# Expert weight loads in eight paced pieces each, with the slot loads between them

## What is computed

```python
xf = layernorm(x).reshape(4096, 512)
gate_scores = xf @ gate_W + gate_b                 # 4 experts
topk_scores, topk_idx = top_k(gate_scores, 2)
weights = softmax(topk_scores)
def expert(w1, bb1, gg1, bbe1, w2, bb2, gg2, bbe2):
    h = relu(_layernorm(xf @ w1 + bb1, gg1, bbe1))
    return _layernorm(h @ w2 + bb2, gg2, bbe2)
out = sum over the two chosen experts of weight * expert(xf); x = x + out + xf
```

## Time and profile before

| | us |
|---|---|
| median of 3 runs (1213.1 to 1216.1) | 1214.87 |
| profiled execution | 1209.59 |
| its span | 1207.8 |
| TensorE busy | 1159.6 |
| VectorE busy | 924.9 |
| ScalarE busy | 731.5 |
| GpSimd busy | 457.2 |
| mean granted TensorE clock | 0.988 of full speed |

### The profile page before, as it was taken

How to read it: one execution, slowest core, us unless ns; L and a number is a source line. 1 busy time by engine, 2 the same in 40 slices (tenths; PEclk the granted TensorE clock), 3 DMA queues, 4 the chain that set the end, 5 groups by cost and what they waited for, 6 DMA issues and landing times.

```text
span 1207.8 us, 24523 instructions
## 1 busy us (share of the span) xinstructions
PE 1159.6 (96%) x6041; PEld 978.9 (81%) x6042; DVE 924.9 (77%) x2196; ACT 731.5 (61%) x2114; POOL 457.2 (38%) x410
## 2 busy tenths in 40 slices
PE   6999999999989999999999998989999999999993
PEld 5788888888878888888888877867888888888882
DVE  6888888887766677877868777678777777777774
ACT  5323333233486757767677662567777777777773
POOL 4040000000052314535445164357655555555543
PEclk9999999999999999999999998899999999999998
DMA  8754544444520302133021358885554444444433
GB/s 271 230 160 160 188 176 146 174 156 165 199 84 1 105 10 97 44 107 104 10 97 44 131 131 227 270 221 122 81 88 81 85 79 86 80 85 80 85 64 42
DMA packets 83237, 143.90 MB, mean 119 GB/s; under 512 B 20460, under 2 KB 24752, under 8 KB 82309
## 3 DMA queue, kind: packets, MB, share of 16 engines
q1 hardware_dynamic: 63872, 101.60, 25.8%
q0 software_dynamic: 18464, 39.14, 17.1%
q10 hardware_dynamic: 837, 2.41, 0.6%
HBM read 78.83 MB, written 67.83 MB: 121 GB/s over the span
## 4 chain that ended last, share of the span: by engine, by line
PE 83%; DMA 5%; DVE 4%; issue 3%; ACT 3%; POOL 2%; POOLq 0%; DVEq 0%; SPq 0%; ACTq 0%
PE banks L1097 27%; PE banks L681 21%; PE banks L746 7%; PE banks L891 6%; PE banks L879 5%; DMA out<-rows,scatter_rows 4%; PE banks L848 3%; PE banks L865 3%; PE banks L1109 2%; PE banks L907 2%; PE banks L1125 2%; ACT rows L1310 2%; PE banks L719 1%; PE banks L800 1%; PE banks L765 1%
## 5 line engine op out<-in xcount | busy, mean ns | idle before, releaser
L1097 PE MATMUL banks<-operands 128*128 x1608 | 388.6, 396 | 10.5 <-DVE operands L1570 5.2
L1097 PEld LDWEIGHTS banks<-operands 128*128 128x128 f32 x1608 | 298.1, 189 | 73.6 <-issue 7.4
L681 PE MATMUL banks<-operands 128*128 128x512 f32 (+2 forms) x1224 | 292.6, 394 | 3.5 <-DVE operands L1570 3.5
L681 PEld LDWEIGHTS banks<-operands 128*128 128x128 f32 (+1 forms) x1224 | 225.6, 192 | 47.8 <-DVE operands L1570 3.7
L1570 DVE TENSOR_TENSOR operands<-banks,operands 128x512 fp32r<-128x512 f32 (+3 forms) x328 | 217.7, 682 | 42.5 <-ACT operands L1189 38.8
L1189 ACT ACTIVATE operands<-banks 128x512 fp32r<-128x512 f32 (+3 forms) x328 | 191.7, 608 | 96.7 <-PE banks L879 45.0
L1310 ACT ACTIVATE rows<-banks,score_shift 128x77 f32<-128x77 f32 x512 | 162.7, 374 | 28.0 <-DVE score_shift L1792 27.2
L1189 ACT ACTIVATE operands<-rows 128x512 fp32r<-128x512 f32 (+3 forms) x79 | 55.3, 709 | 163.8 <-DVE rows L1641 138.1
L1495 ACT ACTIVATE banks<-banks,param_cols 128x128 f32<-128x128 f32 x268 | 99.2, 430 | 82.5 <-PE banks L1125 82.5
L2576 POOL DMA_INDIRECT out<-rows,scatter_rows x67 | 106.6, 1591 | 104.2 <-DVE rows L2315 65.1
L1310 ACT ACTIVATION_READ_ACCUMULATOR rows<-banks,score_shift 128x1 f32 x512 | 129.1, 256 | 0.0
(11 more groups left out here) (178 smaller groups left out, 1707.0 us busy)
## 6 DMA issues: line engine op xcount, KB each, us to landing
expert_parts<-operands SPq DMA_DIRECT2D x32, 512.0 KB, 3.0
operands<-expert_parts SPq DMA_DIRECT2D x8, 2048.0 KB, 11.1
rows<-in_x SPq DMA_DIRECT2D x8, 1024.0 KB, 5.4
rows<-in_L_ffn_W SPq DMA_DIRECT2D x32, 256.0 KB, 3.5
x_rows<-rows SPq DMA_DIRECT2D x8, 1024.0 KB, 4.3
rows<-x_rows SPq DMA_DIRECT2D x8, 1024.0 KB, 5.7
xf_rows<-rows SPq DMA_DIRECT2D x32, 256.0 KB, 2.7
out<-rows SPq DMA_DIRECT2D x32, 256.0 KB, 2.5
```

What stands on the lines that cost most here:

```text
L681: last = nc.tensor.matmul(dst, stationary(a, k), moving(b, k), start=(t == 0 and k == 0), stop=(t == len(terms) - 1 and k == n_k - 1))
L1097: last = nc.tensor.matmul(dst, stationary[:, a, k, :], weights[:, w, bass.ds(e, 1), a2, k, :].rearrange("p e f -> p (e f)"), start=False, ...
```

## The change

Weights 2, 5, 6 and 7 are loaded by a new function `load_expert_parts`: one DMA for each of the eight parts (high or low part a, 128 rows k) of 256 KB. Before the nth is issued, SP waits for the semaphore of the n-1 ahead of it. Four pieces are followed by one pair of slot loads, four more by the next pair. `expert_in` of these weights waits for the count of all eight. Loads 0, 4, 1 and 3 stay as they were. Bytes moved are the same.

```diff
+            def load_expert_parts(s, parts):
+
+                e, w = s // 2, s % 2
+                for n in parts:
+                    a, k = n // KC, n % KC
+                    need(sp, w_in[s], 16 * n)
+                    sp.dma_start(weights[:, w, e, a, k, :].bitcast(F32), ws_d[s, a, k]).then_inc(w_in[s], 16)
+
             def expert_in(s):
-                sp.wait_ge(w_in[s], 16)
+                sp.wait_ge(w_in[s], 16 if s in (0, 4, 1, 3) else 16 * 2 * KC)
                 sp.sem_inc(experts_ready, 1)
...
             expert_in(1)
             load_slot_pairs(5, 7)
-            load_expert(2)
-            load_slot_pairs(7, 9)
+            for half_n in range(2):
+                load_expert_parts(2, range(KC * half_n, KC * (half_n + 1)))
+                load_slot_pairs(7 + half_n, 8 + half_n)
             for s in range(2, 5):
                 expert_in(s)
             for s in range(5, 2 * NE):
-                load_expert(s)
-                load_slot_pairs(2 * s - 1, min(2 * s + 1, EARLY // 2))
+                for half_n in range(2):
+                    pair = 2 * s - 1 + half_n
+                    load_expert_parts(s, range(KC * half_n, KC * (half_n + 1)))
+                    load_slot_pairs(pair, min(pair + 1, EARLY // 2))
                 expert_in(s)
```

## The result

The changed kernel took **1224.14 us** (median of 8 runs, 1218.66 to 1228.18), the kernel before 1216.42 (8 runs, 1213.10 to 1218.51). The ratio is **1.0068, 95% interval 1.0048 to 1.0088**: slower by 7.7 us at the medians, 6 to 11 us by the interval. The prediction had 1218.7 us, a range of 1212 to 1225.5, and a chance of 0.5 for slower by over 0.3%.

The account below looks back on a forecast made before the run. TensorE, busy 96% of the span, was taken as the bound, with 8.0 us lost to late scatter-adds. Terms -8.0 + 0.3 + 7.3 + 2.0 + 2.2 = +3.8 us gave 1218.7 us, range 1212 to 1225.5.

Parts of the forecast that it names:

- The 8.0 us: Time lost between tiles 3 and 10 to scatter-adds slowed by 2 MB weight loads; forecast to go altogether, -8.0.
- The wait for weight 2: TensorE stands in tile 3, before expert 1's first product, until weight 2 has landed: +7.3 us (3.6 to 12.3).
- three pieces at 2.6 us: Landing time taken for three of weight 2's eight pieces, with GpSimd doing nothing until 770.87.
- five at 3.1: Landing time in us taken for weight 2's other five pieces, beside gathers, slot scatters and scatter-adds.
- Clock: TensorE's matmuls after the idle time in tile 3 run at the lower clock for a while: +2.0 us (0 to 3.4).
- Residue: Paced pieces of weights 5 to 7 lengthen scatter-adds and so tiles, 0.2 us a tile: +2.2 us (0 to 6).
- the limit of 5.55: Longest time in us a scatter-add may last before the chain of scatter-adds sets the pace of the tiles.
- The base stores: The burst of the four last base stores moves to wherever SP gets to it and lengthens a tile: +0.3 us.
- The fixed cost: Part of each weight load independent of size: 1.6 us from the landings, about 2.0 us per DMA by the skill.
- The sum: All terms for the whole kernel: -8.0 + 0.3 + 7.3 + 2.0 + 2.2 = +3.8 us.
- the signs listed: Expected in the trace: tile 3 wait 4 to 12 us, pieces 2.5 to 3.6 us, weight 2 whole at about 788.
- rival C: Pieces keep every scatter-add above 5.55 us, making tiles 6.9 us until 861: +7.6 us, 1222.5 us; chance 0.20.

Follow-up runs that it names:

- the repeat: Against the changed kernel, weight 2 whole again, weights 5 to 7 still in paced 256 KB pieces, measured a second time: 1205.37 us, ratio 0.9895 to before.
- the last variant: Against the changed kernel, weight 2 whole, weights 5 to 7 in four paced pieces of 512 KB each: 1211.16 us, ratio 0.9945 to before.

## Why the prediction came out

**Direction and mechanism: right; the size of the wait: too small.** The wait took its place where it was said, in tile 3 ahead of the first product of expert 1, released by SP; removing the pieces of weight 2 alone turns +0.7% into -0.5% or better.

**The 8.0 us: right.** With weights 5 to 7 paced and no wait, 0.4 us are left of them between tiles 3 and 10, 0.9 in the repeat. The scatter-adds fell from 8.9 to between 4.7 and 6.7 us.

**The wait for weight 2: mis-sized,** 7.3 us (3.6 to 12.3) in the sum, 15.3 measured, outside its own ends. The step that failed is the landing time of weight 2's pieces, "three pieces at 2.6 us, as GpSimd does nothing until 770.87" and "five at 3.1". The first three took 3.9, 2.9 and 5.2, 4.2 us more than was said; the other five 2.8, 5.6, 4.4, 2.7 and 2.6, 2.5 us more. There was no quiet stretch for the first three: SP came to weight 2 at 770.94 and not at 765.0, a gather followed at 773.67 and a scatter-add at 776.42. Eight pieces made 30.2 us and not 23.7, 6.5 us of the error; another 1.4 us come from tile 3 being ready 15.1 us behind the first piece (770.94 to 786.05) where it had been 16.5 (765.0 to 781.5). This lead was taken from one profile and is its second weak point: where weight 2 stands at its old place in SP's order, the other profiles have 10.6 to 15.1 us. The run with 2 paced and 5 to 7 whole had a wait of 16.9 us though its eight pieces took only 27.3, since its lead was 10.6. L485's rows had a median of 3.5 and a worst case of 7.9 beside stores; I held the scatter-adds' neighbourhood for milder than that without a row for it. With L485's median for all eight the term would have been 12.

**Clock:** +2.0 was taken, 2.5 measured.

**Residue: too high,** +2.2 against 0.2, and 0.2 more from tile 10 to the last piece. Its first half was right: scatter-adds of 5.0 to 6.3 us beside the pieces, over the limit of 5.55. The second half was not. In the changed kernel they are issued at 814.79, 821.94 and 828.83, 7 us apart, while the tiles go on in steps of 6.35. The chain falls behind the tiles for a while without holding them up. Which slack it uses up (the rows of two tiles have a buffer each) I did not test. The stream itself was taken too short: the 24 pieces took 3.8 us each on average and not 3, and the last landed at 892.4, not at about 861. Nobody waited for them, as forecast.

**The base stores,** +0.3: SP came to them at 892.50, and the tile from 892.94 to 899.72 took 6.78 us, 0.4 over the steady 6.35. About right, and outside the stretch compared above; that the stores are what made this tile longer is not tested.

**The fixed cost.** The Trainium skill (DMA: Bandwidth & Descriptors, Anatomy of one DMA — SWDGE (gpsimd) path) has about 2.0 us per DMA whatever its size, and spoke against the change; in direction it was borne out. The section is on DMAs that GpSimd issues, and these loads are SP's. In size the traces here are above it: beside gathers and scatter-adds 2.2 us (weights 5 to 7) to 3.0 us (weight 2) of a piece were independent of its size.

**The sum:** -8.0 + 15.3 + 2.5 + 0.2 = +10.0 us, which is the stretch from tile 2 to tile 10; +7.7 at the medians, where +3.8 was forecast. The two errors, 8.0 too little and 2.0 too much, partly cancelled. That the time fell into the stated range is in part luck: with the measured wait and all other terms as forecast, the sum is +11.8 and the time 1226.7, above the range's end of 1225.5. Of the signs listed, three did not come as described: the wait is not 4 to 12 us, weight 2 is not whole at about 788 but at 801.1, and pieces take up to 5.6 us. In size the result is rival C's (+7.6), but not by C's mechanism: the tiles are not slowed by the stream.

## What to carry to other kernels

Before a load is cut into pieces that wait for each other, ask for each load by itself when its first reader wants it: here three of the four had 65 us or more to spare when they were loaded whole, and the fourth had 8 us in the profile before (and none in that of the last variant, where TensorE waited 0.3 us for it whole), against a pacing that added over 20. Pace what is early, leave whole what is urgent; that version beat both kernels. A chain of dependent DMAs is priced by the landings seen beside the traffic that will run there, not by the best ones.

## What the runs showed of the hardware

- A 256 KB load landed in 2.5 to 2.9 us while GpSimd issued nothing (six pieces of the changed kernel) and in 2.8 to 5.6 beside its gathers and scatter-adds. Of the weight 2 pieces the three issued within 1.4 us of a scatter-add's start took 4.4 to 5.6. A 512 KB piece beside this traffic took 4.5 us on average for weight 2 and 5.6 for weights 5 to 7, 0.8 and 1.7 more than one of 256 KB.
- A 256 KB load issued 0.5 us behind a 1 MB load by the same engine took 8.8 us in one run and 6.9 in another; other loads were under way as well.
- Beside 24 pieces, one every 3.8 us, scatter-adds took 5.0 to 6.3 us (4.7 to 6.7 in the version with weight 2 whole), where those from 900 to 1150 us of the changed kernel, with no weight load beside them, took 4.6 to 4.9; the whole 2 MB loads raised them to 8.0 to 9.2.
- After 15.3 us without work TensorE ran its next 24 matmuls in 8.2 us in place of 5.7, and was at 2.4 GHz again for the next tile (granted clock 1.00 from 808 on).
